# Graph attention on one core: a second buffer for target scores, more complement counts, and moved mask steps

## The reference, cut to what matters

```python
x = (meta_x @ W).reshape(N, HEADS, DIM)
a_src = jnp.sum(x * att_src, axis=-1)
a_dst = jnp.sum(x * att_dst, axis=-1)
logits = a_src[src] + a_dst[dst]
logits = jax.nn.leaky_relu(logits, NEG_SLOPE)
seg_max = jax.ops.segment_max(logits, dst, num_segments=N)
ex = jnp.exp(logits - seg_max[dst])
seg_sum = jax.ops.segment_sum(ex, dst, num_segments=N)
alpha = ex / (seg_sum[dst] + 1e-16)
msg = x[src] * alpha[:, :, None]
out = jax.ops.segment_sum(msg, dst, num_segments=N)
return out.mean(axis=1) + bias
```

## Time and profile before

| | us |
|---|---|
| median of three runs | 1287.16 |
| lowest and highest | 1284.82, 1287.27 |
| time of the profiled execution | 1286.68 |
| span of the profiled execution | 1284.9 |
| attention stage, first to last masked product | 825.9 to 1274.8 |

### The profile page before, as it was taken

The page is one execution under the profiler, slowest core; times in us unless marked ns, Lnnn a source line. Parts: engine busy times, 40 slices in busy tenths (PEclk is TensorE's granted clock), DMA queues, the critical chain, the costliest instruction groups (busy, mean ns, idle before and its releaser), DMA issues.

```text
span 1284.9 us, 40100 instructions
## 1 busy us (share of the span) xinstructions
PE 1154.3 (90%) x16724; PEld 1074.0 (84%) x16724; DVE 871.6 (68%) x2375; ACT 632.7 (49%) x1161; POOL 62.8 (5%) x113
## 2 busy tenths in 40 slices
PE   0588888888999999999998899599999999999996
PEld 0588888888999999999954899488878888887996
DVE  1899999996443434344642535688878888887887
ACT  0577767661000000000112402578888788788886
POOL 2000000001111111111000002000000000000000
PEclk9866665568999999999999799599999999999998
DMA  1544444420000000000000000000000000000000
GB/s 29 83 71 62 71 61 69 70 51 11 2 3 3 3 3 2 3 3 3 3 2 1 2 3 2 2 2 2 2 2 2 2 2 2 2 2 2 7 12 13
DMA packets 133768, 21.42 MB, mean 17 GB/s; under 512 B 133041, under 2 KB 133458, under 8 KB 133618
## 3 DMA queue, kind: packets, MB, share of 16 engines
q1 hardware_dynamic: 132190, 18.75, 9.7%
q10 hardware_dynamic: 1332, 0.33, 0.1%
q0 software_dynamic: 96, 0.16, 0.0%
HBM read 18.43 MB, written 0.80 MB: 15 GB/s over the span
## 4 chain that ended last, share of the span: by engine, by line
PE 59%; DVE 25%; ACT 7%; issue 6%; DMA 1%; SPq 1%; POOL 0%; DVEq 0%; ACTq 0%; POOLq 0%
PE bank L1786 31%; PE bank L1906 11%; DVE ohk L989 6%; PE bank L1902 6%; ACT Mr L900 4%; DVE ohp L991 4%; DVE Mr L1503 3%; PE bank L1731 3%; DVE raw L979 2%; PE bank L1723 1%; DVE Mr L1510 1%; PE bank L1642 1%; PE bank L1897 1%; DVE oht L949 1%; ACT F L863 1%
## 5 line engine op out<-in xcount | busy, mean ns | idle before, releaser
L1786 PE MATMUL bank<-GH,C 128*128 128x128 f16 x7100 | 397.9, 219 | 0.0
L1786 PEld LDWEIGHTS bank<-GH,C 128*128 128x128 f16 x7100 | 396.9, 98 | 0.1
L1906 PE MATMUL bank<-F,Mr 128*128 128x260 f16 (+1 forms) x2520 | 343.9, 269 | 7.2 <-DVE Mr L1503 3.7
L900 ACT ACTIVATE Mr<-eaT 128x640 f16<-128x640 f32 x433 | 326.5, 822 | 30.0 <-PE bank L1906 28.2
L1906 PEld LDWEIGHTS bank<-F,Mr 128*128 128x128 f16 x2520 | 218.9, 98 | 30.8 <-DVE Mr L1503 4.3
L1503 DVE TENSOR_TENSOR Mr<-Mr,C 128x640 f16<-128x640 f16 x433 | 195.2, 485 | 72.9 <-ACT Mr L900 71.2
L1902 PE MATMUL bank<-FN,C 128*128 128x130 f16 x2260 | 210.0, 220 | 0.8 <-DVE r L1411 0.8
L747 ACT ACTIVATE plo<-bank 128x256 f32<-128x256 f32 (+1 forms) x84 | 30.2, 361 | 362.7 <-PE bank L1786 346.6
L1148 DVE TENSOR_TENSOR S<-bank,plo 128x256 f32<-128x256 f32 (+1 forms) x84 | 33.2, 395 | 210.7 <-ACT plo L747 210.7
L1902 PEld LDWEIGHTS bank<-FN,C 128*128 128x128 f16 x2260 | 164.2, 98 | 10.5 <-DVE r L1411 1.4
L1642 PE MATMUL bank<-ohk,ohp 128*128 128x100 f16 (+3 forms) x1452 | 159.9, 270 | 3.0 <-DVE ohp L991 3.0
(11 more groups left out here) (250 smaller groups left out, 959.6 us busy)
## 6 DMA issues: line engine op xcount, KB each, us to landing
raw<-in_edges_dram SPq DMA_DIRECT2D x242, 68.0 KB, 2.1
xs<-in_x_dram SPq DMA_DIRECT2D x1, 800.0 KB, 4.1
out_dram<-xs SPq DMA_DIRECT2D x4, 160.0 KB
wg<-in_L_gnn_W_dram ACTq DMA_DIRECT2D x2, 64.0 KB
z<-in_L_gnn_att_src_dram SPq DMA_DIRECT2D x1, 128.0 KB, 2.7
z<-in_L_gnn_att_dst_dram SPq DMA_DIRECT2D x1, 128.0 KB, 3.0
out_dram<-xs SPq DMA_DIRECT2D x1, 128.0 KB
wts<-in_L_gnn_W_dram ACTq DMA_DIRECT2D x4, 16.0 KB
```

Of the source, the lines that this page charges most:

```text
L900: act.activation(Mr[:, mi % RB, :], nadS, ACT.Sigmoid, bias=steep[:, h, t:t + 1], scale=-STEEP / XS).then_inc(s_step, 1)
L1786: last = pe.matmul(bank[:, b, jj * 2 * D:(jj + 1) * 2 * D], C[:, t, (t0 + jj) * P:(t0 + jj + 1) * P], GH[:, par, t, :], start=t == 0 and j ...
L1906: return pe.matmul(bank[:, k, a_:z_], Mr[:, mi % RB, j * P:(j + 1) * P], F[:, t, a_:z_], start=start, stop=t == T - 1)
```

## The change

It has five parts.

1. `nadS` becomes a pair of buffers used in turn; the second lies over weights and norms that the attention stage no longer needs, which are put into one tile (`cold`). With it, `nad` moves from unit 21 to unit 17 and no longer waits for the masks; it waits for the copy of this block's scores, and for the `scaled` steps which read the same PSUM bank.
2. `apart` names 113 units instead of 48. Blocks 1, 2 and 3 of heads 0 to 2 have 8 (before 6, 6 and 4), first blocks of heads 1 to 3 have 4 (0), last blocks of heads 0 to 2 have 3 (0), blocks 1 to 4 of the last head have 5 (0). The very first block still has none.
3. The compares on VectorE go from 67 units to 45: blocks 1 to 3 of heads 0 to 2 have 2 instead of 5, the same blocks of the last head 1 instead of 2, first and last blocks 3 instead of 2. The other masks begin with a step on ScalarE.
4. `take` and `evicted` move from unit 3 to unit 5 in the queues of ScalarE and VectorE, and `post` from unit 4 to unit 6.
5. In the first block, and once in the fourth blocks, steps that make features come some units earlier.

```diff
+    STT_FIRST = (8, 14, 20)
+    STT_ENDS = ((8, 14, 21), (3, 9, 19))
+    STT_MID = ((8, 17), (17,))
+    APART_MID = (1, 4, 7, 10, 13, 16, 19, 22)
+    APART_ENDS = ((5, 12, 19, 22), (1, 7, 19))
+    APART_LAST = (1, 4, 7, 19, 22)
+    NADS = 17
...
-        nadS = eaT[:, TP // 2 + VW:TP // 2 + VW + NG * P]
+        nadS = (eaT[:, TP // 2 + VW:TP // 2 + VW + NG * P], cold[:, 0:NG * P])
...
         def by_act(h, b, t):
-            return t % 10 != 8 if h == H - 1 or b in (0, NG - 1) else t % 5 != 3
+            return t not in (STT_FIRST if (h, b) == (0, 0) else STT_ENDS[b // (NG - 1)] if b in (0, NG - 1) else STT_MID[h == H - 1])
...
         def apart(h, b, t):
-            return h < H - 1 and (b in (1, 2) and t % 4 == 0 and t < T - 1 or b == 3 and t % 7 == 0)
+            return (h, b) != (0, 0) and t in (APART_LAST if h == H - 1 and b else APART_ENDS[b // (NG - 1)] if b in (0, NG - 1) else APART_MID)
...
+        def scaled_by(blk):
+
+            h, b = blk // NG, blk % NG
+            return h * NG + (NG if b < NG - 2 else NG + 2 if h < H - 1 and b == NG - 2 else NG + 3 if h < H - 1 else NG)
...
                     act.wait_ge(s_nad, blk + 1)
-                    act.activation(nadS, pnad, ACT.Copy).then_inc(s_nads, 1)
+                    if blk >= 2:
+                        act.wait_ge(s_M, (blk - 1) * T)
+                    act.activation(nadS[blk % 2], pnad, ACT.Copy).then_inc(s_nads, 1)
...
-                            if t == 3 and blk:
+                            if t == 5 and blk:
                                 take((blk - 1) // NG, (blk - 1) % NG)
-                            if blk == 0 and t in (1, 6, 13, 18):
-                                high_f(0, (t + 9) // 6)
+                            if blk == 0 and t in (1, 6, 11, 16):
+                                high_f(0, (t + 4) // 5)
...
-                            if t == 3 and blk:
+                            if t == 5 and blk:
                                 evicted((blk - 1) // NG, (blk - 1) % NG)
-                            if t == 4 and blk:
+                            if t == 6 and blk:
                                 post((blk - 1) // NG, (blk - 1) % NG)
                             if blk == 0:
-                                if t in (5, 12, 17):
-                                    scaled(0, (t + 7) // 6)
-                                elif t in (2, 7, 14, 19):
-                                    low_f(0, (t + 8) // 6 if t > 2 else 1)
+                                if t in (5, 10, 15):
+                                    scaled(0, (t + 5) // 5)
+                                elif t in (2, 7, 12, 17):
+                                    low_f(0, (t + 3) // 5)
...
-                            if b == NG - 2 and h < H - 1 and t in (10, 18):
-                                scaled(h + 1, (t - 10) // 8)
+                            if b == NG - 2 and h < H - 1 and t in (10, 15):
+                                scaled(h + 1, (t - 10) // 5)
...
-                            if blk == 0 and t in (2, 7, 12):
-                                xw(0, 2 + t // 5, blk)
+                            if blk == 0 and t in (2, 6, 10):
+                                xw(0, 2 + t // 4, blk)
...
-                            if t == T - 4 and (h, b) != (H - 1, NG - 1):
-                                pe.wait_ge(s_M, (blk + 1) * T)
+                            if t == NADS and (h, b) != (H - 1, NG - 1):
+                                pe.wait_ge(s_nads, blk + 1)
+                                pe.wait_ge(s_vx, scaled_by(blk))
                                 nad(h + (b + 1) // NG, (b + 1) % NG)
```

25 lines of the change are left out of this document (13 added, 12 removed).

## The result

The changed kernel takes 1299.20 us (median of 9 runs, 1298.04 to 1301.13). The kernel before, beside it on the same chip, takes 1285.46. The ratio is 1.0101 with a 95% interval of 1.0085 to 1.0117, so the change makes the kernel 1% slower. The forecast was 1278.8 us and 0.86 for faster. The profiled execution took 1299.21 with a span of 1297.4; that is 12.5 us over the span before.

A forecast was written before the change was run, and what follows sets the result against it. TensorE was taken as the bound, with some 14 us of waits to win. Gains 16.9 + 7.9 + 3.5 = 28.3 less losses 11.3 + 5.4 + 2.0 + 1.5 = 20.2 gave net 8.1, so 1278.8 us; range 1264 to 1285.

The forecast's parts named there:

- Evictions behind the fifth mask: At block heads, `take` moved behind steps that could be done anyway: 2 us lost, bounds 0 and 4.
- the waits for mask 6 and behind: Head of 13 blocks: TensorE waits 0.87 us each behind `post`, 11.3 us lost; stalls after it, 5.4 us lost.
- rival (a): Block heads: waits behind the one complement buffer are not there; 1262.1 us, or 1270.5 with half; chance 0.27.
- `nad`: Attention stage: with the second buffer TensorE no longer waits for masks in front of `nad`; 7.9 us gained.
- complements: TensorE in the attention stage: each of 65 more complement units saves 0.26 us; 16.9 us gained, bounds 9 and 16.9.
- Rival (d): TensorE: a narrow product goes no faster than its weight load, so 65 units save 4 us; 1291.7 us; chance 0.02.
- compares and feature steps: Mainly first blocks of heads: moving them removes TensorE's waits for compares (2.8 us) and some for products (0.7); 3.5 gained.
- the 1.5 for features: First and last blocks: VectorE's features share with more complements; 0.25 x 6 = 1.5 us lost, bounds 0 and 6.
- (b): First and last blocks of heads 0 to 2: VectorE becomes the bound where it makes features; 1283.0 us; chance 0.09.
- (c): Middle blocks: VectorE's side work doesn't fit between products at ScalarE's pace; 1294.8 us with half unhidden; chance 0.07.

The follow-up runs named there:

- latecmp: The changed kernel with five compares (units 8, 11, 14, 17, 20) instead of two in the nine middle blocks; 1301.72 us, ratio 1.0127.
- take3: The changed kernel with `take` and `evicted` put back to unit 3 and `post` to unit 4; 1267.55 us, ratio 0.9858.
- noap4: The changed kernel without the complement of unit 4 in the 13 blocks with complements at units 1 and 4; 1283.20 us, ratio 0.9982.
- post5: The changed kernel with `post` moved from unit 6 to 5, `take` and `evicted` staying at 5; 1281.52 us, ratio 0.9963.
- oldap: The changed kernel with the 48 complement units of before instead of 113; 1285.51 us, ratio 0.9994.
- best_a: The changed kernel with `take` and `evicted` at unit 3, `post` at 4, and the first block's compares and feature steps as before; 1266.34 us, ratio 0.9847.
- take4: The changed kernel with `take` and `evicted` at unit 4 and `post` at unit 5; 1270.75 us, ratio 0.9890.

## Why the prediction was wrong

**The step that failed: "Evictions behind the fifth mask".** I had 2.0 us, bounds 0 and 4; it is 18.9 by shown gaps and 21.5 by starts. I wrote that step 5 needs the buffer for which `take` waits, so that `take` moves "behind steps that could be done anyway". That a step *may* be done isn't that there is *time* for it. ScalarE's 0.72 a step is as slow as TensorE's unit in line, and slower than its units with complements; with the copy (0.7) it can't make five steps of the new block before TensorE is through with the old, even from a full ring (latecmp). At three steps it has 0.31 us to spare (take3), at four it is 0.5 late, at five 1.24, and with the 0.94 to TensorE's second bank that makes 1.03 in a middle block. Undoing it alone, with the rest of the change in place, gives 31.6 us. Some 20 are the evictions (22.8 by starts, 2.3 in take3). The rest is mask 6 and its train, since `post` goes back too. For the last blocks of heads, with the compare at unit 3, I had 0.2 to 0.3 of wait; it is 0.89 to 1.01, by VectorE.

In my sum I had asked when the first eviction could start by TensorE, 0.72 behind its last product, a row of the kernel before with three steps in front. What I should have counted was ScalarE's own work behind its last wait. The rows had it: seven times 0.717 is 5.0 us for step 24, the copy and five steps, and the last six units, two of them with complements, take TensorE at most 4 x 0.72 + 2 x 0.58 = 4.0.

**Right: the waits for mask 6 and behind.** 13 x 0.93 = 12.1 by starts against 13 x 0.87 = 11.3, in the blocks named, behind the instructions named. noap4 and post5 each take them away by another end of the same chain. What comes behind is 5.2 against 5.4: 0.18 at unit 8 in each of the nine middle blocks, as forecast, and in the last head 0.42 (forecast 0.5) at unit 8 and 0.42 to 0.63 (forecast 0.45) at unit 10. The shown gaps have only 2.3 of it, as most are too short. The worth of the whole, 17.7 in post5, is close to 16.7. Not all of the train hangs on mask 6: take3 still waits 1.9 at unit 10. So rival (a), that these waits are not there, is out, although it had 0.27.

**Right: `nad`.** All 13 waits are gone, 7.9 us by the gaps and 10.0 by starts, and ScalarE waits at no copy. Alone the buffer is worth 11.7, since the lead helps elsewhere. I had not priced that.

**Right: complements.** Without waits the stage from block 1 on takes 404.5 us before and 386.5 after; oldap, which differs from the changed kernel in the complements alone, has 404.3. That is 17.8 for 65 complements, 0.27 each, where I had 0.26. All kernels here with 48 complements lie between 403.8 and 404.5, all with 113 between 386.3 and 387.9. It holds in the last head too. From its head to the next, block 17 (it is the one called 16 in the earlier trace rows) takes 21.59 us before, with no wait, and 23.02 after, with 2.78 of waits by starts (1.01, 0.93, 0.42 and 0.42): five complements save 1.35. By the shown gaps of these four waits, 0.85, 0.77, 0.26 and 0.26, it looks like 0.70, or 0.14 each; the other 0.64 are the four times 0.16 that these leave out. Rival (d), a narrow product bound by its weight load, is out: it had 0.06 each. The rule cited from the Trainium skill, page "TensorE: Matmul & The Clock Gate", section "Back-to-back issue gap", would give 5 x 0.017 = 0.09 a complement (5.5 us for all 65; the 5.6 of the prediction is a slip). The measured 0.27 disagrees, and the measurement decides.

**Wrong: compares and feature steps, -3.5 forecast, +0.2 by shown gaps, and with the 1.5 for features +2.0 by starts against -2.0.** The compare gaps of 0.93 in first blocks went, but gaps of 0.62 in front of a product came in their place. ScalarE and TensorE in the changed kernel's block 5:

```profile
957.95 0.76 ACT L876 ACTIVATE F<-Vx 128x650 f16<-128x650 f32 x1 [2.10 <-DVE Vx L1409]
...
960.00 0.73 PE L1921 MATMUL bank<-F,Mr 128*128 128x260 f16 x5 [0.62 <-DVE Mr L1518]
```

ScalarE's `high_f` (L876) waits 2.10 us for VectorE's `scaled` (L1409), the steps behind it come late, and TensorE gets its mask 0.62 too late. The stage's first block now waits 2.2 us where, `nad` aside, it waited 1.0. best_a shows that putting its steps back gives 1.8 us there.

**Rivals (b) and (c).** (b) had VectorE close to full in first and last blocks of heads: they come in at 24.39 and 22.91 with VectorE busy for some 20.5, and take3's at 23.86 and 21.85, the latter with TensorE full. So first blocks are held back by gaps that remain (0.62, and in take3 0.68 as well), last ones aren't. (c), side work that doesn't fit between ScalarE's steps, is out: take3 holds all 113 complements in middle windows of 19.87. It would have had the right sign, for a wrong reason; no rival of mine had the engine that turned out late.

By ScalarE's rows a step takes 0.82 alone and comes every 0.72 in a row. The Trainium skill, page "ScalarE: Activation LUTs", section "What ACT_TABLE_LOAD costs", gives for one with a pointer bias about 280 ns + 0.833 ns an element and an overlap of 93 ns; for 640 that is an estimate of 0.813 and 0.720. The trace agrees, so the pace that decided this case could be had from either.

**Open.** How to order the gaps away that are left in take3 (8.7 us, of which 2.1 stand in the stage's first block and some 3 x 1.3 in the first blocks of heads 1 to 3). A second complement buffer wasn't tried.

## What to carry to other kernels

When a step moves back in a queue, count from that engine's last wait: everything between it and the step, at the engine's own pace, against what the consumer still has to do until it needs the result. A full ring is the most lead there is, and a pace only equal to the consumer's never adds to it; here two steps of 0.72 us turned 0.3 us of slack into 1 us of wait, on average, in each of 19 blocks. Look at both queues of a hand-over, and move one back only as far as the later of them allows.

A bundle of edits can hide a winner: the change without its fourth part is worth 19 us here, and the complements without the buffer lose 20.

The idle time that a profile shows for an engine whose instructions overlap is a lower bound. Where it is subtracted from a span to get at the work that is left, count from start to start.

## What was not expected of the hardware

Little: the engines kept their pace in all kernels. The signals between them are short and steady. From the end of TensorE's last masked products to a `take` that is there in time pass 0.20 us (take3), and from the first eviction's start to TensorE's next bank 0.40 to 0.41 (after, take4, latecmp). I had not expected that lateness of an engine at the end of a block would be so exact: 1.24 us in the changed kernel and in latecmp. It is the same difference in both, 5.07 - 3.83, since both have a full ring at step 24.
